# A two-layer recurrence on one core: GpSimd takes over a semaphore's lowering, and one sum gets a third buffer

## The reference

```python
def layer(x, h0, Wx, Wh, b):                 # x: (8, 1024, 512)
    xW = einsum('ntd,dh->nth', x, Wx) + b
    h_next = tanh(h_prev @ Wh + xw_t)        # for each of the 1,024 steps
    return all h
x = x + layer(x, cond, L0_Wx, L0_Wh, L0_b)
x = x + layer(x, cond, L1_Wx, L1_Wh, L1_b)
```

## Time and profile before

| | us |
|---|---|
| median of 3 runs | 2039.12 |
| lowest, highest | 2035.76, 2039.52 |
| the profiled execution's own time | 2037.84 |
| its span | 2035.8 |

### The profile page before, as it was taken

How to read it: one execution, slowest core, us unless ns; L and a number is a source line. 1 busy time by engine, 2 the same in 40 slices (tenths; PEclk the granted TensorE clock), 3 DMA queues, 4 the chain that set the end, 5 groups by cost and what they waited for, 6 DMA issues and landing times.

```text
span 2035.8 us, 251040 instructions
## 1 busy us (share of the span) xinstructions
PE 2020.9 (99%) x110552; PEld 1838.4 (90%) x110552; DVE 1866.6 (92%) x12254; ACT 1524.0 (75%) x7426; POOL 862.2 (42%) x4090
## 2 busy tenths in 40 slices
PE   8999999999999999999999999999999999999999
PEld 6999999999999999999999999999999999999997
DVE  5999999999999999999999999999999999999997
ACT  4777777777777777777777777777777777777776
POOL 5444444444444444444444444444444444444442
PEclk9999999999999999999999999999999999999999
DMA  3000000000100000100000000000001010100000
GB/s 108 24 28 24 28 24 28 24 28 24 28 24 28 24 28 24 28 24 28 24 28 24 28 24 28 24 28 24 28 24 28 24 28 24 28 24 28 24 27 18
DMA packets 112015, 56.75 MB, mean 28 GB/s; under 512 B 12432, under 2 KB 111008, under 8 KB 111520
## 3 DMA queue, kind: packets, MB, share of 16 engines
q1 hardware_dynamic: 111168, 53.53, 9.2%
q10 hardware_dynamic: 576, 1.18, 0.2%
q0 software_dynamic: 32, 0.02, 0.0%
HBM read 37.90 MB, written 16.78 MB: 27 GB/s over the span
## 4 chain that ended last, share of the span: by engine, by line
PE 99%; issue 0%; DVE 0%; DMA 0%; ACT 0%; ACTq 0%
PE ps_rec L295 39%; PE ps_rec L277 37%; PE ps_xw L249 22%; DMA bias<-b_in 0%; ACT h L418 0%; DVE zt L516 0%; PE ps_rec L342 0%; DVE x_mid L553 0%; DVE z L528 0%; ACTq L470 0%; ACT ps_xw L381 0%; DVE x_out L562 0%; ACTq L478 0%
## 5 line engine op out<-in xcount | busy, mean ns | idle before, releaser
L204 POOL TENSOR_TENSOR h<-h 128x8 f32<-128x8 f32 x4064 | 845.3, 208 | 1150.4 <-ACT h L418 991.5
L295 PE MATMUL ps_rec<-wh_part,h 128*32 128x128 bf16 (+1 forms) x60984 | 1172.5, 216 | 0.7 <-issue 0.7
L277 PE MATMUL ps_rec<-wh,h 128*32 128x128 f32 (+1 forms) x33008 | 1129.1, 255 | 8.6 <-ACT h L418 5.0
L418 ACT ACTIVATE h<-z 128x16 f32<-128x16 f32 x4066 | 720.8, 216 | 483.9 <-DVE z L528 356.1
L295 PEld LDWEIGHTS ps_rec<-wh_part,h 128*32 128x32 bf16 x60984 | 915.3, 97 | 112.5 <-issue 0.9
L516 DVE STREAM_TRANSPOSE zt<-ps_rec 128x64 f32<-128x64 f32 x4096 | 778.7, 228 | 76.8 <-PE ps_rec L277 12.6
L407 ACT ACTIVATE ps_rec<-xw,mask 128x128 f32<-128x128 f32 x2040 | 726.9, 356 | 0.9 <-issue 0.6
L277 PEld LDWEIGHTS ps_rec<-wh,h 128*32 128x32 f32 (+1 forms) x33008 | 648.6, 105 | 76.3 <-ACT h L418 14.0
L528 DVE TENSOR_REDUCE z<-zt 128x16 f32<-128x48 f32 x4066 | 664.1, 202 | 2.5 <-DVE zt L516 1.5
L204 DVE TENSOR_TENSOR h<-h 128x16 f32<-128x16 f32 x2034 | 372.7, 183 | 75.3 <-ACT h L418 0.5
L249 PE MATMUL ps_xw<-wx,x_pe 128*32 128x128 f32 x8240 | 320.2, 273 | 1.4 <-ACT ps_xw L381 1.4
(11 more groups left out here) (23 smaller groups left out, 23.6 us busy)
## 6 DMA issues: line engine op xcount, KB each, us to landing
x_pe<-x_t SPq DMA_DIRECT2D x256, 64.0 KB, 1.9
x_dve<-x_t SPq DMA_DIRECT2D x256, 64.0 KB, 2.0
out_t<-x_out SPq DMA_DIRECT2D x256, 64.0 KB, 1.7
wh<-wh_in SPq DMA_DIRECT2D x1, 1024.0 KB, 4.8
wx<-wx_in SPq DMA_DIRECT2D x1, 1024.0 KB, 9.1
wx<-wx_in ACTq DMA_DIRECT2D x1, 512.0 KB, 5.1
wx<-wx_in SPq DMA_DIRECT2D x1, 512.0 KB, 4.8
wh<-wh_in SPq DMA_DIRECT2D x1, 512.0 KB, 7.2
```

The lines of the kernel that those rows point to most:

```text
L204: return eng.tensor_tensor(step[:, tiles, to], step[:, tiles, of], h_bits(l, n)[:, tiles, of], ALU.subtract)
L277: mm = pe.matmul(out, state, wh[l][:, k, g * P:(g + 1) * P][:, cols], start=False, stop=k == KC - 1 and is_whole(l, n), skip_group_check=True,
L295: mm = pe.matmul(rows(ps_rec[l][n % 2], g)[:, cols], h_bits(l, n - 1)[:, k, :], wh_part[l][:, i, at:at + P][:, cols], start=False, stop=k ...
L418: act.activation(h_of(l, n)[:, tiles, :], src[:, tiles, :], ACT.Tanh).then_inc(h_count(l, n)[0], 1)
```

## The change

GpSimd does the lowering, behind its own two rests of the step, and VectorE no longer does. `x_mid` has three buffers, and `sum_mid` waits for `out_done` only once in four steps, for the whole group that last used the buffer.

```diff
+MIDS = 3
...
-        x_pe, x_dve, x_mid, x_out = ([sb(f"{name}{j}", [P, GRP]) for j in range(2)]
-                                     for name in ("x_pe", "x_dve", "x_mid", "x_out"))
+        x_pe, x_dve, x_out = ([sb(f"{name}{j}", [P, GRP]) for j in range(2)] for name in ("x_pe", "x_dve", "x_out"))
+        x_mid = [sb(f"x_mid{j}", [P, GRP]) for j in range(MIDS)]
...
-            return xs[n // S4 % 2][:, :].rearrange("p (k s b) -> p s k b", s=S4, b=B)[:, n % S4]
+            return xs[n // S4 % len(xs)][:, :].rearrange("p (k s b) -> p s k b", s=S4, b=B)[:, n % S4]
...
-                act.activation(xm_pe[:, :], x_mid[c % 2][:, :], ACT.Copy).then_inc(xm_done, 1)
+                act.activation(xm_pe[:, :], x_mid[c % MIDS][:, :], ACT.Copy).then_inc(xm_done, 1)
...
         def _(pool):
...
+            def lower(l, n):
+
+                if (n + LAG * l) % PAIR == 0 and is_split(l, n - 1):
+                    for i in range(2 - l):
+                        done, count = split_count(l, n - 1, i)
+                        pool.sem_inc(done, -count)
+
             for l, n in ORDER:
                 if is_split(l, n):
...
                     rest(pool, l, n, 2, tiles).then_inc(split_count(l, n, 1 - l)[0], PAIR if (l, n) == (0, PARTED - 1) else 1)
+                    lower(l, n)
...
-            def lower(l, n):
-
-                if (n + LAG * l) % PAIR == 0 and is_split(l, n - 1):
-                    for i in range(2 - l):
-                        done, count = split_count(l, n - 1, i)
-                        dve.sem_inc(done, -count)
-
             def sum_mid(n):
 
                 c, t = n // S4, n % S4
-                if n >= 2 * S4:
-                    dve.wait_ge(out_done, n - 2 * S4 + 1)
+                if t == 0 and c >= MIDS:
+                    dve.wait_ge(out_done, S4 * (c - MIDS + 1))
                 dve.wait_ge(*h_count(0, n))
...
                     turn(0, n0)
-                    lower(0, n0)
                     total(0, n0)
...
                     turn(1, n1)
-                    lower(1, n1)
                     total(1, n1)
```

## The result

The changed kernel takes 2030.47 us (median of 7 runs, 2029.1 to 2031.52), the kernel before in the same comparison 2036.81 us (7 runs, 2035.76 to 2039.52). The medians are 6.3 us apart. The ratio is 0.9965, 95% interval [0.9954, 0.9977]: 7 us less, between 4.7 and 9.4. The forecast was 2031.0. The profiled execution after took 2030.24 us.

A forecast was written before the change was run, and what follows sets the result against it. The prediction took TensorE to bound the ordinary 1.95 us slot. From the profiled 2037.84 us it took 6.9 for VectorE (7.9 lost less 1.0 remaining) and added 0 for GpSimd: 2030.9, taken as 2031.0 us, range 2028.8 to 2036.5.

The forecast's parts named there:

- TensorE bounds the ordinary slot: Steady loop: the chain of waits runs through TensorE alone, 1.95 us a slot, so less VectorE work saves nothing there.
- All the gain is in the late slots: Long middle part, 1,012 slots: some 7.9 us are lost in single late slots, all that the change can win there.
- The cause is the packet's border behind a sequencer instruction: VectorE's queue: a pause of about 0.36 us at each 128-instruction code packet shows where a sequencer instruction took the lead.
- The lowering's 3.95: VectorE, behind both layers' lowerings: the 3.95 us lost there goes when the lowering leaves VectorE.
- `sum_mid`'s 3.34: VectorE, behind `sum_mid`'s wait for `out_done`: the 3.34 us lost there goes, but for the quarter where the wait stays.
- The remainder: VectorE after the change: 0.97 us still lost, behind `sum_mid`'s remaining wait, behind `sum_out`, and at the `out_free` wait.
- GpSimd takes it for nothing: GpSimd's gaps of 0.52 and 0.38 us ahead of its rests take in the lowerings and packet pauses: cost 0.
- Half of it: Rival, chance 0.10: on VectorE the loss behind `sum_mid`'s wait stays and only 3.9 us goes, giving 2033.9 us.
- The pauses merely move: Rival, chance 0.10: VectorE's 99 remaining packet places cost today's mean 0.068 us, losing 6.7 us, giving 2036.6 us.
- GpSimd's pauses: Rival, chance 0.06: 44 packet pauses on GpSimd delay layer 1's rests and TensorE, up to +15.8 us, giving 2046.8 us.

The follow-up runs named there:

- ten more on GpSimd: The changed kernel with ten more semaphore instructions on GpSimd behind each lowering: 2252.03 us in one execution.
- the row of five kernels: The changed kernel with the lowering back on VectorE and 0, 1, 2, 4 or 7 sequencer instructions added ahead of the loop: 2039.08, 2031.74, 2031.57, 2033.98, 2038.81 us.
- the shifted kernel: The changed kernel with one more sequencer instruction at the head of VectorE's queue: 2029.1 us in one execution.
- the kernel whose waits are carried: The changed kernel with two x_mid buffers, `out_done` awaited every step, and VectorE's second waits moved onto transpositions without a wait: 2028.99 us.
- the run with two buffers: The changed kernel with two x_mid buffers and the wait for `out_done` in every step, lowering still on GpSimd: 2032.68 us.
- the first experiment: The changed kernel with the lowering back on VectorE, three x_mid buffers kept: 2039.08 us, ratio to the kernel before 1.0003.

## Why the prediction was right

**TensorE bounds the ordinary slot**: holds. The slot is 1.95 us in both, and in every kernel of the study but the one with ten more on GpSimd.

**All the gain is in the late slots**: holds. The middle stretch fell by 6.96 us, 6.9 was forecast. The profiled execution fell by 7.6: 6.96 there, 1.4 at the start, where executions differ by more than that among themselves, and 0.8 back in what lies outside the span.

**The cause is the packet's border behind a sequencer instruction**: shown by the row of five kernels (2.4 to 9.6 us lost with the same slots), by the sum for `x_mid` in the shifted kernel (0.22 us with a wait ahead of it, nothing without), and at that same sum by the kernel whose waits are carried. What the sequencer does in the pause no run shows; that it has to do with the next packet of code rests on the distance of 128, on the packets' 8.2 KB and on their number, which followed the queues' lengths.

**The two terms.** The lowering's 3.95 measured 4.1 (8.0 less the 3.9 of the run with two buffers). Of `sum_mid`'s 3.34, 0.48 was to stay, so 2.86 was forecast, and about 2.9 came. The remainder, 0.97 by forecast, is 1.0: 0.86 at two of the three places named, nothing at the third, and ScalarE's 0.08, which the forecast's list left out. It had luck in it: my count of the queue was off by two, and since the changed kernel's pattern has only an even and an odd set of places, an error of two does nothing. With 56 instructions in four slots, as in the first experiment, the same error put the sizes out by 2 to 6 us. The term was right; the count that it rests on was not.

**GpSimd takes it for nothing**: holds. A lowering there follows the last in 0.083 us, where VectorE's 0.10 was taken. Of its 44 packet borders none made a slot late beyond those that VectorE explains.

**The rivals.** *Half of it* is out: once the lowering was gone, the third buffer and its rarer wait brought 2.9 us. *The pauses merely move* is out, since 98 borders lost 1.0 and not 6.7. The Trainium skill, Runtime: NRT & Kernel Launch, section on instruction fetch mechanics, speaks of blocks of 256 instructions at a cost that is mostly hidden; here the borders are 128 apart and cost up to 0.26 us each where the sequencer has no lead. *GpSimd's pauses* needs about four more instructions behind each lowering to show at all, and ten to be dear.

## What to carry to other kernels

On an engine whose program is written out in full, count sequencer instructions (second waits, semaphore changes) as well as busy time: each takes away the sequencer's lead, and the pause at the next packet of code then lands on the engine. Put a second wait on a neighbouring instruction that has none (this cost nothing in the one kernel that did it), and semaphore upkeep on an engine with gaps. And when an edit moves a bound kernel by a few tenths of a per cent, shift the program by an instruction or two before believing in a cause: here that alone was worth 7 us.

## What the runs showed of the hardware

- Semaphore instructions on GpSimd start 0.083 us apart (0.078 in long rows), on VectorE 0.10.
- The pause at a packet's border is some 0.36 us (two lowerings 0.45 apart instead of 0.10), and it came at each 128th instruction of VectorE's queue wherever the place could show it. On GpSimd it is 0.29 us (0.37 apart instead of 0.08).
- The loss per border depends on the place so steadily that a table read in one kernel gave another's loss to within 0.6 us in eight kernels, once the queue was counted rightly (for three of them only after their result). What I had not expected is the size of the swing: from 2.4 to 9.6 us by one to seven instructions that do nothing.
